# Where VectorE writes the transposed selection within a pass of a three-layer graph-attention kernel, before or behind the messages

## What is computed

```
h = (x @ W).reshape(N, 8, 32)
e = leaky_relu(el[src] + er[dst])
ex = exp(e - m[dst])
a = ex / segment_sum(ex, dst)[dst]
out = segment_sum(h[src] * a, dst) + b
```

## Time and profile before

| what | value |
|---|---|
| median of 3 runs | 7141.27 us (7137.47 to 7150.18) |
| the profiled execution | 7151.61 us, its span 7149.9 us |
| PE busy | 5616.7 us (79%) |
| DVE busy | 4514.0 us (63%) |
| POOL busy | 4535.0 us (63%) |
| ACT busy | 1582.9 us (22%) |
| mean granted clock of PE | 0.895 of full speed |
| selT, L1133 | 1322 instructions, 487.8 us |
| gathers, L434 | 4716, 4521.7 us |

### The profile page before, as it was taken

The page is one execution under the profiler, slowest core; times in us unless marked ns, Lnnn a source line. Parts: engine busy times, 40 slices in busy tenths (PEclk is TensorE's granted clock), DMA queues, the critical chain, the costliest instruction groups (busy, mean ns, idle before and its releaser), DMA issues.

```text
span 7149.9 us, 149324 instructions
## 1 busy us (share of the span) xinstructions
PE 5616.7 (79%) x35000; PEld 4505.8 (63%) x35001; DVE 4514.0 (63%) x11249; ACT 1582.9 (22%) x4666; POOL 4535.0 (63%) x4739
## 2 busy tenths in 40 slices
PE   4687777777776777777777777999999988888767
PEld 2566656555554666555555556888888777776546
DVE  5677766666555667766665556555666666667664
ACT  2111111000000000000000004555555444433212
POOL 0677777777776677777777775344444455666774
PEclk9788888888877888888888778999999999999989
DMA  4555555555554445455554443222223333444442
GB/s 170 180 148 151 152 150 153 149 145 146 145 142 130 135 140 149 143 146 148 145 145 142 141 133 100 74 78 80 84 84 90 92 95 102 115 118 129 138 134 84
DMA packets 386097, 916.19 MB, mean 128 GB/s; under 512 B 130561, under 2 KB 192777, under 8 KB 385930
## 3 DMA queue, kind: packets, MB, share of 16 engines
q0 software_dynamic: 227904, 681.63, 34.8%
q1 hardware_dynamic: 115530, 194.09, 8.2%
q10 hardware_dynamic: 42624, 40.02, 1.7%
HBM read 871.89 MB, written 43.49 MB: 128 GB/s over the span
## 4 chain that ended last, share of the span: by engine, by line
PE 30%; POOL 27%; issue 23%; DVEq 7%; DVE 6%; DMA 2%; ACTq 2%; ACT 2%; POOLq 1%; SPq 0%
POOL gat L434 27%; PE bank L1516 11%; PE bank L1428 7%; PE looked_up L1439 5%; PE bank L1439 5%; DVEq L265 2%; DMA gat<-table,meta 2%; ACTq L265 1%; DVE sel L1176 1%; PE bank L1382 1%; DVE selT L1133 1%; ACT L524 1%; DVEq L1176 1%; DVE lg L1156 1%; DVEq L1156 1%
## 5 line engine op out<-in xcount | busy, mean ns | idle before, releaser
L434 POOL DMA_INDIRECT gat<-table,meta x4716 | 4521.7, 959 | 2477.3 <-issue 1363.9
L1516 PE MATMUL bank<-msg,sel 128*128 x10536 | 3192.0, 454 | 919.9 <-DVE sel L1176 902.8
L1516 PEld LDWEIGHTS bank<-msg,sel 128*128 128x128 f32 x10536 | 2187.7, 218 | 1380.0 <-issue 1002.2
L1166 DVE SCALAR_TENSOR_TENSOR msg<-bank,gat 128x1056 f32 x1317 | 1654.0, 1256 | 263.6 <-ACT bank L568 250.8
L568 ACT ACTIVATE bank<-lg 128x32 f32<-128x32 f32 x1317 | 262.0, 199 | 4556.4 <-DVE lg L1160 4402.3
L1176 DVE TENSOR_TENSOR sel<-iota_t,meta 128x256 f32<-128x256 f32 x2634 | 1004.2, 419 | 45.3 <-PE bank L1516 38.2
L1482 PEld LDWEIGHTS looked_up<-uvb,selT 128*128 (+1 forms) x10584 | 485.5, 99 | 685.0 <-issue 601.7
L1482 PE MATMUL looked_up<-uvb,selT 128*128 (+1 forms) x10584 | 543.0, 173 | 395.5 <-DVE selT L1133 385.3
L1156 DVE TENSOR_TENSOR lg<-gat,looked_up 128x64 f32 x878 | 193.3, 220 | 960.4 <-POOLq L441 787.1
L1428 PEld LDWEIGHTS bank<-xT,w 128*128 128x128 f32 x6272 | 750.5, 192 | 15.8
L1428 PE MATMUL bank<-xT,w 128*128 128x128 f32 x6272 | 759.6, 276 | 0.0
(11 more groups left out here) (231 smaller groups left out, 2821.3 us busy)
## 6 DMA issues: line engine op xcount, KB each, us to landing
dstb<-dst_lists SPq DMA_DIRECT2D x297, 512.0 KB
gat<-table,meta POOLq DMA_INDIRECT x4716
table<-hrow ACTq DMA_DIRECT2D x98, 140.0 KB
w<-in_W SPq DMA_DIRECT2D x2, 4096.0 KB
table<-hrow SPq DMA_DIRECT2D x49, 140.0 KB, 1.8
region<-xnT_d ACTq DMA_DIRECT2D x50, 128.0 KB
region<-qT_d ACTq DMA_DIRECT2D x50, 128.0 KB
res<-in_x SPq DMA_DIRECT2D x1, 6272.0 KB, 25.3
```

The lines of the kernel that those rows point to most:

```text
L434: pool.indirect_dma_start(gat[:, r, c, :], None, table[l], bass.IndirectOffsetOnAxis(meta[:, m, c, 0:1].bitcast(U32), 0)).then_inc(s_done, 16)
L1166: dve_v.scalar_tensor_tensor(msg[:, bass.ds(n % 2, 1), :, :].rearrange("p a c (h d) -> p (a c) h d", h=H), ex_p.unsqueeze(3).to_broadcast( ...
L1516: last = pe.matmul(acc[:, 0:MSG], sel[:, c, :], msg[:, bass.ds(m % 2, 1), c, :].rearrange("p a m -> p (a m)"), start=opens and c == 0, sto ...
```

## The change

`logits` no longer ends with `selectT` in layers 0 and 1. A new function `select_later` calls it with the same slot, tile, semaphore and place, behind `messages` and ahead of `select` (at a tile's opening also ahead of `tile_slots` and `divide`). In layer 2 all stays. No instruction is added or removed.

```diff
@@ logits @@
                     dve_v.tensor_tensor(lg[:], lg2[:, :, 0:H], lg2[:, :, H:UV], ALU.max).then_inc(logit_ready[l], 1)
-                    selectT(g_next, T_next, selT_ready[l], n % 2 if l + 1 < LAYERS else 0)
+                    if l + 1 == LAYERS:
+                        selectT(g_next, T_next, selT_ready[l], 0)
+
+                def select_later(T, g, n):
+
+                    if l + 1 < LAYERS:
+                        selectT(g, T, selT_ready[l], n % 2)
@@ pairs @@
                     logits(T, first, n_first, first + later, T, True)
                     messages(first, n_first)
+                    select_later(T, first + later, n_first)
                     if l + 1 < LAYERS:
                         end1, end2, last, g_next, unshared = tile_slots(dve, T, (5, 10))
...
                         logits(T, g, n, g_later, T_later)
                         messages(g, n)
+                        select_later(T_later, g_later, n)
                         select(g, n, slot_done[l])
...
                     logits(T, last, n_last, g_next + (later - 1), T + 1)
                     messages(last, n_last)
+                    select_later(T + 1, g_next + (later - 1), n_last)
                     select(last, n_last, tile_last[l])
```

## The result

| | before | after |
|---|---|---|
| median of 4 runs, us | 7140.19 (7137.47 to 7150.18) | 7265.08 (7263.94 to 7268.9) |
| span of the profiled execution, us | 7149.9 | 7262.3 |

The changed kernel takes 1.0173 [1.0156, 1.0191] of the time: 125 us more, slower as forecast, but more than twice the 58 us of the forecast and outside its range.

The account below looks back on a forecast made before the run. DVE, with the PE and ACT steps it awaits, was taken to bound two short-tile stretches, POOL's gathers the long tiles. Terms 10 + 28 + 5 + 13 + 2 made 58 us on 7141: 7199 us, range 7152 to 7234.

Parts of the forecast that it names:

- In front of `msg`: Each pass on DVE: `msg` already starts as early as ACT's exponentials allow, so taking `selT` away there gains 0.
- Behind `msg`: Each pass on DVE: `selT` now stands between `msg` and `sel`, making `sel` 0.30 us later.
- Lookups then aggregate: PE's order: late lookups, taken at 0.7 us, precede the aggregate, which starts 1.1 us behind `sel` instead of 0.62.
- Layer 0's bound tiles: Short layer-0 tiles where DVE sets the end: +0.35 us at opening, +0.3 in last pass, 0.65 per tile, 10 in all.
- Layer 1's bound tiles: Short layer-1 tiles where DVE sets the end: 0.35 + 0.65 + 0.6 + 0.3 = 1.9 us per tile, 28 in all.
- the pass before the last, +0.6: Layer-1 bound tile: later `sel` and aggregate delay transpose, copy and exponentials; +0.6 us taken, not 0.8, for shorter queued lookups.
- The mixed stretch of layer 1: Layer-1 tiles where POOL waits now and then: some 13 tiles at half a tile's cost, 1.0 us each, 13 us.
- The long tiles of layer 1: Tiles where POOL's gathers set the pace: later `sel` hidden under DVE's 2.17 us wait per pass, so 0 per pass.
- The rival of the clock: Shorter PE pause at openings keeps 2.4 GHz, 1.8 us less in each of 45 tiles: -23 us, 7118 us; chance 0.08.
- "PE becomes the bound": Rival: at 1.2 GHz `sel` waits for PE's lookups and aggregate, 30 to 45 us more, 7235 us; chance 0.09.
- "Covered": Rival: DVE's waits for ACT and PE take back its loss, leaving 11 us, 7152 us; chance 0.13.
- The chances: Odds of outcome: slower 0.80, same 0.12, faster 0.08, with half of covered and all of clock under 0.2%, 14 us.

Follow-up runs that it names:

- e4: Kernel before with one more DVE compare of `selT`'s size behind each `msg` of layers 0 and 1, output unread, `selT` still in front: 7187.13 us, 1.0066.
- e8: Changed kernel with PE's three register loads of a tile's opening moved in front of its lookups: 7278.24 us, 1.0187.
- e12: Changed kernel with filler matmuls of zeros, six at the openings and eight in layer 1 as in e2: 7220.32 us, 1.0109.
- e6: Kernel before with the same layer-1 fillers as e2, as its control: 7132.93 us, 0.9982.
- e2: Changed kernel with eight matmuls of zeros in layer 1 before lookups of the first loop's passes and the last two passes: 7223.88 us, 1.0118.
- e3: Kernel before with `selT` behind the messages only in the pass before each tile's last: 7211.06 us, 1.0100.
- e9: Kernel before with both kinds of fillers, twelve at the openings of layers 0 and 1 and eight in layer 1's passes: 7110.88 us, 0.9958.

## Why the prediction was right and wrong

**In front of `msg`: right.** The forecast gained nothing there. ACT's exponentials end at 2447.09 + 0.20 = 2447.29, and `msg` starts 0.18 us behind them, as it did before.

**Behind `msg`: right.** `selT` starts 1.17 us behind `msg` and `sel` 0.26 behind that (2447.47, 2448.64, 2448.90), against a forecast of 0.30. Both start before the one in front has ended. The Trainium skill, "VectorE: DVE Perf Modes", The DRAIN you can't avoid, has the next instruction wait until the pipeline is empty, and adds that one which is not held starts earlier. The prediction took up only the first half, by which the gap would be the full 0.34 us; this trace agrees with the second.

**Lookups then aggregate: right in most passes, too low in one.** The aggregate starts 2449.83 - 2448.90 = 0.93 us behind `sel`, forecast 1.1. But in the pass before the last it is 1.27 us in the mean of the 15 tiles, against 0.57 before, because the lookups take 0.97 us there and not 0.7. The prediction called the 0.98 us of the earlier trace rows lookups "at the low clock" and took less for a mix of both levels; the clock there was full:

```profile
277.00:279.00 2.00, 0.98 (x12) 0.71 (x12) 1.61 (x2) 0.20 (x1) 1.39 (x3) 1.00 0.35 101
```

**Layer 0's bound tiles: right in their terms.** 12.1 us over 14 tiles are 0.86 per tile against 0.65. In the mean `msg` of the second pass comes 0.34 us later behind the opening (forecast 0.35), and the next opening 0.28 later behind the last `msg` (forecast 0.3); the passes between, forecast at nothing, lose 0.23. The spread was not foreseen: 0.07 to 2.3 us per tile. Of layer 0's 26 us, 8 are DVE's later `sel` (e4). How the rest divides between the later lookups, the opening's chain and the lower clock of the last pass stays open; e8 and e12 were meant to tell and do not.

**Layer 1's bound tiles: the step that failed.** The forecast was 0.35 + 0.65 + 0.6 + 0.3 = 1.9 us per tile; 48.3 / 15 = 3.2 was measured. Cut at the same places, means of the 15 tiles in us, worked out from the traces:

| part of a tile | forecast | before | after | before, filled (e6) | after, filled (e2) |
|---|---|---|---|---|---|
| opening to `msg` of the second pass | +0.35 | 7.86 | 8.23 | 7.86 | 8.22 |
| from there to `attend` | +0.65 | 7.08 | 7.79 | 6.85 | 7.40 |
| to `msg` of the pass before the last | | 2.10 | 2.04 | 2.07 | 2.04 |
| **to `msg` of the last pass** | **+0.6** | **4.75** | **6.67** | **4.68** | **5.71** |
| to the next opening | +0.3 | 3.14 | 3.42 | 3.14 | 3.42 |

Three of the four terms came out within 0.1 us. The one that failed is the pass before the last, +0.6: it measured +1.92. With the pauses filled in both kernels (e6 to e2) it is +1.03, which is the 0.3 us of the later `sel` and the 0.7 us (0.57 to 1.27) that the aggregate starts later behind it; the prediction had added these to 0.8 and taken 0.6. The other 0.9 is the clock: the sum added waits to durations of before (2.04 us at 2536.94) and let these stand, while this aggregate grew by 0.74 us in the mean. Moved alone, the same pass measured 2.1 per tile (e3).

**The mixed stretch of layer 1: mis-sized.** "Some 13 tiles" at 1.0 us were counted from POOL's waits of before, 12 of which are for the landing of a gather and not for DVE; it was 20 tiles at 1.6. A tile that grows by more than DVE's spare time becomes bound even where it was not, and DVE's waits for POOL, which the forecast let halve the price, were more than half used up (56.4 to 23.1 us in these tiles). The long tiles of layer 1, forecast at 1 us, lost 11, and 7 with filled pauses (1045.3 - 1038.2); the reason is open.

**The rival of the clock had the mechanism with the wrong sign.** It said that a shorter pause at the opening would free the first aggregate, and in 9 of the 15 tiles of layer 1 it is free. What it overlooked is that with `selT` behind `msg` PE makes lookups and aggregate in one block behind one longer pause: 86.7 us in front of the lookups, 1.8 us each, where short lookups had broken the pause before. No such wait is longer than 2.5 us, and still the level falls. The low clock left a place where nobody waited and came to one where ACT and DVE wait. One such block per tile is enough for it: e3 has nearly the same aggregates and the same 0.81. That the filled pauses give time back is shown; why the low level falls on just these passes is argued. In layer 0 the first aggregates stayed at 3.9 us. The Trainium skill, "TensorE: Matmul & The Clock Gate", HAM oscillation, has pauses between bursts throttle the next burst; e2 agrees with that, since filling the pauses brought the clock from 0.81 to 0.88.

**"PE becomes the bound" did not come.** `sel` waits for PE only 5.0 us in all in layer 1's bound stretch, by the waits of the trace, as before. **"Covered" fell** by POOL's waits, which grew by the whole loss of the stretch.

**The chances.** They put all of the clock's case under 0.2%, but its 23 us are 0.3% of 7141.

## What to carry to other kernels

When one engine's small job moves, the order of the engine that it feeds moves with it: here twelve short matmuls that had kept PE's pause in two went into one block with the large ones, and at one place in the tile that cost 1.0 us by order and 0.9 by the clock. Do not round a sum of waits down where it stands on the chain. The durations of a clocked engine are not constants of a forecast; ask of each burst what the engine does in front of it and who waits for its end, since low clock costs nothing where nobody waits and its full length where a chain does. And where the tile that grows feeds a fixed-rate engine, count the tiles that become bound, not those that are.

## What the runs showed of the hardware

- Matmuls of zeros keep the clock up: eight of them with 254 columns in bf16 take 1.03 us and gave back 37 us in layer 1 of the changed kernel; with twelve more at the openings the kernel before reached a clock of 0.97 in layer 1's bound stretch, and 0.9958 of its time in all.
- Pauses of PE of at most 2.5 us brought the 1.2 GHz level: the changed kernel has a clock of 0.81 from 2298 to 2720 us, and its longest pause there is 2.54 us.
- The mean clock says little on its cost. e3 and the changed kernel both have 0.81 in layer 1's bound stretch, at 405 and 422 us, and e9 with 0.97 is only 2 us shorter there than e6 (367.1 and 369.1).
- The same register load of DVE's sequencer at an opening (L265) takes 1.18 to 1.20 us in most tiles of layers 0 and 1 and 0.60 to 0.64 in every fourth, in both kernels. Before, tiles 5 and 9 of layer 0 took 22.4 to 22.5 us against 24.05 of tile 3; after, all three took 24.1 to 24.3, and the shorter load gained nothing there.
